# Odd tokens moved by a ladder matmul, and the diagonal block of a causal filter split in late and early outputs

## The reference, cut to what matters

```python
x = x + conv(_ln_c(x))                 # deformable 3x3 convolution, batch norm, SiLU; x is (4, 64, 32, 32)
t = _to_tokens(x)                      # (4, 1024 tokens, 64)
t = t + ffn(_ln_t(t))                  # spectral unit, below
x = _from_tokens(t, x)

# ffn, for u of (b, t, d), 16 filters phi_k, 4 branches over 1, 1/2, 1/4, 1/8 of the tokens
U_plus  = causal_conv(phi_k, u)        # by FFT in the reference
U_minus = (-1)^t * causal_conv(phi_k, (-1)^t * u)
out  = einsum('btkd,k,kde->bte', U_plus, s, Mpp) + einsum('btkd,k,kde->bte', U_minus, s, Mpm)
out += sum over lags 0..2 of u[t - lag] @ Mu[lag]
```

## Time and profile before

| | |
|---|---|
| median of 3 runs | 545.5 us (543.98 to 546.7) |
| the profiled execution | 545.57 us, of which the span of its records is 543.4 us |
| PE busy | 439.2 us, 81% of the span |
| DVE busy | 316.9 us, 58% |
| POOL busy | 296.8 us, 55% |
| ACT busy | 206.4 us, 38% |
| mean granted PE clock | 0.90 of 2.4 GHz |
| pass starts (L944 or first wait of the loop) | 110, 158, 208, 267, 332, 374, 425, 482 us; the end of the last is at 540 us |

### The profile page before, as it was taken

One profiled execution on the slowest core, in us unless ns is written; L12 is line 12 of the kernel. 1 busy time (PEld: TensorE's weight loads), 2 busy tenths in 40 slices (PEclk: granted clock), 3 DMA queues, 4 the chain that ended last, 5 costly groups with the idle time before them and its releaser, 6 DMA issues.

```text
span 543.4 us, 7147 instructions
## 1 busy us (share of the span) xinstructions
PE 439.2 (81%) x2660; PEld 217.9 (40%) x2660; DVE 316.9 (58%) x768; ACT 206.4 (38%) x413; POOL 296.8 (55%) x295
## 2 busy tenths in 40 slices
PE   4986481438775995999989996976699699989997
PEld 3442441315443442444434342643344354534333
DVE  5759977999864959292738429677374934040000
ACT  2124120125543562434333343654356244424232
POOL 1067777778777777777777773777776000000000
PEclk9999595558897999799989998889699889999999
DMA  6943699832334333333333332333433000000000
GB/s 154 185 109 106 155 326 349 259 111 83 102 102 112 102 98 109 103 104 103 104 109 98 104 100 53 104 93 108 114 103 97 6 10 1 2 5 11 0 1 10
DMA packets 47746, 54.41 MB, mean 100 GB/s; under 512 B 28656, under 2 KB 38134, under 8 KB 47713
## 3 DMA queue, kind: packets, MB, share of 16 engines
q0 software_dynamic: 13824, 37.77, 23.6%
q1 hardware_dynamic: 27865, 13.94, 10.2%
q10 hardware_dynamic: 6024, 2.26, 1.9%
HBM read 50.12 MB, written 3.30 MB: 98 GB/s over the span
## 4 chain that ended last, share of the span: by engine, by line
PE 58%; DVE 24%; DMA 10%; issue 3%; ACT 2%; SPq 1%; DVEq 0%
PE bank L902 32%; DMA u<-u 9%; PE bank L919 7%; PE bank L848 3%; PE bank L779 3%; DVE G L459 3%; PE bank L838 3%; DVE sil L472 2%; PE bank L760 2%; DVE G L460 2%; PE bank L939 2%; PE bank L876 1%; DMA filt<-in_L_ffn_phi_dram 1%; DVE V L463 1%; DVE st L299 1%
## 5 line engine op out<-in xcount | busy, mean ns | idle before, releaser
L279 POOL DMA_INDIRECT G<-corner_table,idx x288 | 294.2, 1022 | 122.0 <-issue 86.2
L902 PE MATMUL bank<-filt,u 128*128 128x512 f16 x960 | 243.2, 397 | 46.5 <-DMA u<-u 38.4
L680 ACT COPY u_conv<-bank 64x512 f32<-64x512 f32 x256 | 148.3, 579 | 202.7 <-PE bank L902 198.7
L902 PEld LDWEIGHTS bank<-filt,u 128*128 128x128 f16 x960 | 89.5, 100 | 167.8 <-issue 49.9
L919 PE MATMUL bank<-u_conv,mixw 128*64 128x256 f32 (+1 forms) x640 | 79.2, 356 | 5.9 <-issue 5.9
L459 DVE TENSOR_TENSOR G<-G,bank 128x2304 f32<-128x2304 f32 x32 | 81.5, 2547 | 1.3 <-DMA G<-corner_table,idx 1.2
L463 DVE TENSOR_TENSOR V<-G 128x576 f32<-128x576 f32 x32 | 24.4, 761 | 67.9 <-PE bank L839 67.2
L919 PEld LDWEIGHTS bank<-u_conv,mixw 128*64 128x64 f32 x640 | 35.8, 137 | 52.1 <-issue 50.6
L460 DVE TENSOR_TENSOR G<-G 128x1152 f32<-128x1152 f32 x32 | 43.5, 1358 | 1.1
L471 DVE TENSOR_SCALAR expo<-expo 128x128 f32<-128x128 f32 x16 | 4.4, 274 | 59.4 <-ACT expo L654 59.1
L838 PE MATMUL bank<-ident_swap,V 128*128 128x128 f32 x128 | 22.3, 309 | 14.6 <-DVE V L463 12.1
(11 more groups left out here) (153 smaller groups left out, 308.5 us busy)
## 6 DMA issues: line engine op xcount, KB each, us to landing
filt<-filter_rows SPq DMA_DIRECT2D x16, 514.0 KB, 12.2
G<-corner_table,idx POOLq DMA_INDIRECT x288
corner_table<-n_uT SPq DMA_DIRECT2D x12, 128.0 KB, 3.5
mixw<-in_x_dram SPq DMA_DIRECT2D x2, 512.0 KB, 6.3
filt<-in_L_ffn_M_phi_plus_dram SPq DMA_DIRECT2D x4, 256.0 KB, 7.5
out_dram<-o_sb ACTq DMA_DIRECT2D x8, 128.0 KB, 2.0
filt<-n_L_ffn_M_phi_minus_dram ACTq DMA_DIRECT2D x2, 256.0 KB, 5.6
corner_table<-n_uT ACTq DMA_DIRECT2D x4, 128.0 KB, 4.8
```

Source lines behind the costliest of these rows:

```text
L279: pool.indirect_dma_start(G[:, k, tap, :], None, corners[bp], bass.IndirectOffsetOnAxis(ap=idx[:, q % 2, k, tap:tap + 1], axis=0)).then_in ...
L680: act.copy(u_conv[C * par:C * par + C, g % 2, :, b2, p, :], conv_ps[par][rows].rearrange("c (k a) -> c k a", k=GROUP)).then_inc(conv_copie ...
L902: last = pe.matmul(conv_ps[par][:].rearrange("c (k a) -> c k a", k=GROUP), u16[:, NJ * bp + j2, hl, b2, par:par + 2].rearrange("s w c -> s ...
```

## The change

- **Moving the odd tokens.** The two SP DMAs and the memsets of slot 2 go. `ladder` is a 128x256 f16 matrix with an identity in columns 127 to 254 and zeros beside it, made by DVE at the start. In step 0 of a pass, ahead of the diagonal block, PE multiplies the chunk's odd tokens (and, for j > 0, those of the chunk before) with a slice of it: one or two matmuls of 256 columns into `conv_ps[1]`. ACT casts the result into slot 2 of `u16` (128x256), casts a 64x128 part into `u_early`, and copies 64x256 of `u16` into `u_early` as well. PE waits for the first two of these (`u_shifted`) ahead of all of step 1, and for the third (`early_ready`) inside step 2.
- **The order of steps.** `i` now gives group, then `par`, then image; the bank goes by the image, so that two steps in a row are the two images with the same filters.
- **The diagonal block.** It is triangular: the early 64 output tokens take nothing from the late 64 tokens. From step 2 on, the three diagonal matmuls of a step give only the 64 late outputs of each filter (256 columns, all 128 tokens). The early outputs of both images are made in the even step: three matmuls of 256 columns with the 64 early tokens of image 0 (partitions 64 to 127) into bank 0, each followed by one with the 64 early tokens of image 1, which `u_early` holds on partitions 0 to 63, into bank 1. The even step therefore waits in its middle for ACT to have emptied bank 1, and the odd step no longer waits for it. Steps 0 and 1 stay whole.

```diff
-            sp.wait_ge(shift_zeroed, BP)
-            for q in range(NQ):
-                sp.wait_ge(u_ready, 2 * q + 2)
-                sp.dma_start(u16[0:P - 1, q, :, :, 2], u16[1:P, q, :, :, 0]).then_inc(u_shifted, 16)
-                if q % NJ:
-                    sp.dma_start(u16[P - 1:P, q, :, :, 2], u16[0:1, q - 1, :, :, 0]).then_inc(u_shifted, 16)
...
-            for q in range(0, NQ, NJ):
-                dve.memset(u16[3 * P // 4:P, q, :, :, 2], 0.0).then_inc(shift_zeroed, 1)
+            dve.memset(ladder[:, 0:P - 1], 0.0)
+            dve.memset(ladder[:, 2 * P - 1:2 * P], 0.0)
...
+            dve.wait_ge(s_ident, 16)
+            dve.tensor_copy(ladder[:, P - 1:2 * P - 1], ident).then_inc(ladder_ready, 1)
...
-                g, b2, par = i // 4, i // 2 % 2, i % 2
+                g, par, b2 = i // 4, i // 2 % 2, i % 2
...
+            def copy_stepped(n):
+
+                act.wait_ge(u_stepped, n + 1)
+                stepped = conv_ps[1][:, 0:4 * C].rearrange("s (h b c) -> s h b c", h=2, b=2)
+                act.copy(u16[:, n, :, :, 2], stepped).then_inc(u_shifted, 1)
+                act.copy(u_early[:, :, 2], stepped[C:P, :, 1]).then_inc(u_shifted, 1)
+                act.copy(u_early[:, :, 0:2], u16[C:P, n, :, 1, 0:2]).then_inc(early_ready, 1)
+
             for n in range(NQ):
+                copy_stepped(n)
...
+                def step_odd_tokens():
+
+                    pe.wait_ge(u_ready, 2 * n + 2)
+                    pe.wait_ge(conv_copied[1], START + STEPS * n)
+                    dst = conv_ps[1][:, 0:4 * C].rearrange("s (h b c) -> s h b c", h=2, b=2)
+                    last = pe.matmul(dst, ladder[:, P:2 * P], u16[:, n, :, :, 0], start=True, stop=(j == 0))
+                    if j:
+                        last = pe.matmul(dst, ladder[:, 0:P], u16[:, n - 1, :, :, 0], start=False, stop=True)
+                    last.then_inc(u_stepped, 1)
...
-                    pe.wait_ge(conv_copied[par], START + STEPS * n + 2 * (i // 2))
+                    if not (split and b2):
+                        pe.wait_ge(conv_copied[b2], START + STEPS * n + 2 * (i // 2))
                     for j2 in range(j + 1):
                         if j2 == j and i == 0:
-                            pe.wait_ge(u_ready, 2 * n + 2)
-                        if j2 == j and i == 1:
-                            pe.wait_ge(u_shifted, 16 * (7 * bp + 2 * j + 1))
+                            step_odd_tokens()
+                        if j2 == 0 and i == 1:
+                            pe.wait_ge(u_shifted, 2 * (n + 1))
                         lag = P * (j - j2)
+                        a0 = C if split and j2 == j else 0
...
+                    if split and b2 == 0:
+                        if i == 2:
+                            pe.wait_ge(early_ready, n + 1)
+                        pe.wait_ge(conv_copied[1], START + STEPS * n + 2 * (i // 2))
+                        for e, (hl, part) in enumerate(products):
+                            last = pe.matmul(out_of[0][:, :, 0:C], u16[C:P, n, hl, 0, par:par + 2].rearrange("s w c -> s (w c)"),
+                                             filt_h[C:P, ks, par, part, 2:2 + C], start=False, stop=(e == 2), skip_group_check=True)
+                            pe.matmul(out_of[1][:, :, 0:C], u_early[:, hl, par:par + 2].rearrange("s w c -> s (w c)"),
+                                      filt_h[0:C, ks, par, part, 2 + C:2 + P], start=(e == 0), stop=False, skip_group_check=True)
```

More of the change, by code:

```diff
@@ L77, in metaformer_kernel @@
         off_bias = sb("off_bias", [P, NOFF])
+        ladder = sb("ladder", [P, 2 * P], F16)
+        u_early = sb("u_early", [C, 2, 3, C], F16)
         w_off = sb("w_off", [P, TAPS, NCH])
@@ L184, in metaformer_kernel @@
         conv_copied = [sem(f"conv_copied{i}") for i in range(2)]
-        shift_zeroed, u_shifted, mix_scaled = sem("shift_zeroed"), sem("u_shifted"), sem("mix_scaled")
+        early_ready = sem("early_ready")
+        ladder_ready, u_stepped, u_shifted, mix_scaled = sem("ladder_ready"), sem("u_stepped"), sem("u_shifted"), sem("mix_scaled")
         group_mixed, mixed_copied, pass_turned = sem("group_mixed"), sem("mixed_copied"), sem("pass_turned")
@@ L672, in copy_products @@
             def copy_products(n, i):
-                g, b2, par = i // 4, i // 2 % 2, i % 2
+                g, par, b2 = i // 4, i // 2 % 2, i % 2
                 if i % 4 == 0 and N_GROUPS * n + g >= 2:
                     act.wait_ge(group_mixed, N_GROUPS * n + g - 1)
-                act.wait_ge(conv_done[par], STEPS // 2 * n + i // 2 + 1)
+                act.wait_ge(conv_done[b2], STEPS // 2 * n + i // 2 + 1)
                 for p in range(2):
@@ L680, in copy_products @@
                     act.copy(u_conv[C * par:C * par + C, g % 2, :, b2, p, :],
-                             conv_ps[par][rows].rearrange("c (k a) -> c k a", k=GROUP)).then_inc(conv_copied[par], 1)
+                             conv_ps[b2][rows].rearrange("c (k a) -> c k a", k=GROUP)).then_inc(conv_copied[b2], 1)
             def store_pass(n):
@@ L862, in _ @@
             pe.wait_ge(ones_ready, 2)
+            pe.wait_ge(ladder_ready, 1)
             for r in range(2):
@@ L886, in _ @@
                           for s in range(seg0, seg0 + nseg)]
-                def convolve(i):
-                    g, b2, par = i // 4, i // 2 % 2, i % 2
+                def step_odd_tokens():
[6 more added lines that the diff above has]
+                    last.then_inc(u_stepped, 1)
+                def convolve(i):
+                    g, par, b2 = i // 4, i // 2 % 2, i % 2
+                    ks = slice(GROUP * g, GROUP * g + GROUP)
+                    products = ((0, 0), (0, 1), (1, 0))
+                    split = i >= 2
+                    out_of = [b[:].rearrange("c (k a) -> c k a", k=GROUP) for b in conv_ps]
                     if n == 0 and i % 4 == 0:
@@ L900, in convolve @@
                         lag = P * (j - j2)
-                        for e, (hl, part) in enumerate(((0, 0), (0, 1), (1, 0))):
-                            last = pe.matmul(conv_ps[par][:].rearrange("c (k a) -> c k a", k=GROUP),
+                        a0 = C if split and j2 == j else 0
+                        for e, (hl, part) in enumerate(products):
+                            last = pe.matmul(out_of[b2][:, :, a0:P],
                                              u16[:, NJ * bp + j2, hl, b2, par:par + 2].rearrange("s w c -> s (w c)"),
-                                             filt_h[:, GROUP * g:GROUP * g + GROUP, par, part, lag + 2:lag + 2 + P],
-                                             start=(j2 == 0 and e == 0), stop=(j2 == j and e == 2))
@@ L906, in convolve @@
-                    last.then_inc(conv_done[par], 1)
+                                             filt_h[:, ks, par, part, lag + 2 + a0:lag + 2 + P],
+                                             start=(j2 == 0 and e == 0 and not (split and b2)), stop=(j2 == j and e == 2), skip_group_check=True)
+                    if split and b2 == 0:
+                        if i == 2:
+                            pe.wait_ge(early_ready, n + 1)
+                        pe.wait_ge(conv_copied[1], START + STEPS * n + 2 * (i // 2))
+                        for e, (hl, part) in enumerate(products):
+                            last = pe.matmul(out_of[0][:, :, 0:C], u16[C:P, n, hl, 0, par:par + 2].rearrange("s w c -> s (w c)"),
+                                             filt_h[C:P, ks, par, part, 2:2 + C], start=False, stop=(e == 2), skip_group_check=True)
+                            pe.matmul(out_of[1][:, :, 0:C], u_early[:, hl, par:par + 2].rearrange("s w c -> s (w c)"),
+                                      filt_h[0:C, ks, par, part, 2 + C:2 + P], start=(e == 0), stop=False, skip_group_check=True)
@@ L908, in mix @@
+                    last.then_inc(conv_done[b2], 1)
                 def mix(k):
```

## The result

The changed kernel takes 505.34 us (median of four runs, 504.82 to 506.99), the kernel before beside it 545.71: ratio 0.9269, 95% interval 0.9236 to 0.9301, 7.3% faster. All ratios in this text are to the kernel before, run beside the version in question. The forecast was 504.4.

The account below looks back on a forecast made before the run. PE was taken as bound by the moved-token DMA (9.1% of the span, about 49 us) and the low clock behind it. Gathers cap the gain at 37.2 until pass 6, plus 3.95 behind: 545.57 - 41.15 = 504.4 us, range 500 to 516.

Parts of the forecast that it names:

- up to k=10 of pass 2: Passes 0 to 2: gathers hold k=10 of pass 2 to 240.3 against 248.66; 8.35 less 1.0 for clock, gain 7.35 us.
- starts of passes 3 to 7: Pass starts without the DMA wait, at full clock: gains 4.15, 5.35, 9.9, 6.55 and 1.25, sum 27.2 us.
- other pairs: Remaining step pairs with split diagonal: 0.9 us in rest of pass 2, 1.8 each in passes 3, 5, 6, 7; 8.1.
- rest of pass 4: Pass 4 after its start: no gain; pairs some 0.4 us longer, hidden by PE's 2.61 us wait for DVE at k=10.
- taken by the gathers at pass 6: k=10 of pass 6 not before 426.4, so gain there at most 37.2 against 38.7 us summed: gathers last by 1.5.
- The new chain: Pass start: PE may begin step 1 about 1.1 us after u_ready and step matmuls; 0.3 us waiting replaces the DMA.
- The pair: Two steps' diagonal: six 256-column matmuls 0.65 us plus half-row ones 0.32 side by side, against 1.30; 0.30 us saved per pair.
- rival 1: Half-row matmuls run one after the other, pairs save nothing: gain 33.3, 512.2 us; chance 0.17.
- The rule on weight loads: Skill page's 107 ns per 128-column load: six loads would fill 0.64 us and the pair save nothing; forecast sided against it.
- rival 2: Gathers hold more, POOL wins nothing back: k=10 of pass 6 at 434.2, gain 33.4, 512.2 us; chance 0.10.
- rival 3: Even step's wait for bank 1 bites with j = 1 and more: 0.5 us in 42 pairs, 21 us, 525; chance 0.06.
- rival 4: Small f16 matmuls cost 0.216 us each, pairs 1.3 dearer: 566 us, slower than before, deciding from 0.17 each; chance 0.03.

Follow-up runs that it names:

- e3_dma_order: Kernel before with only the new order of steps, keeping the DMA (waited for at step 2) and whole diagonal blocks: 526.21 us, ratio 0.9632.
- e8_ladder_old_order: Ladder alone, with steps and banks ordered as in the kernel before and whole diagonal blocks: 508.48 us, ratio 0.9301.
- e1_no_split: Changed kernel with ladder and new order, but whole diagonal blocks in all steps and no copies into u_early: 510.29 us, ratio 0.9343.
- e4_same_rows: Changed kernel with image 1's early half taken from the same 64 rows as image 0's: 515.69 us, ratio 0.9439.
- e7_filler: Changed kernel with unread filler matmuls on PE ahead of k=10 in passes 0, 1 and 4: 505.94 us, ratio 0.9279.
- e6_whole_j0: Changed kernel with whole diagonal blocks in passes 0 and 4: 503.26 us, ratio 0.9253.
- e11_after_again: The changed kernel itself, unedited, run again beside the later runs: 505.66 us, ratio 0.9255; its profiled execution took 507.28.
- e9_finish_first: Changed kernel with DVE's finish(q,0) moved ahead of weigh(q,1,1), so it doesn't stand behind the unit's last gathers: 496.53 us, ratio 0.9084.

## Why the prediction was right, and which of its steps were not

| term | forecast gain | in the two traces |
|---|---|---|
| up to k=10 of pass 2 | 7.35 | 7.74 |
| starts of passes 3 to 7 | 27.2 | 25.9 |
| other pairs | 8.1 | 5.6 |
| rest of pass 4 | 0 | -0.84 |
| taken by the gathers at pass 6 | -1.5 | 0 |
| sum | 41.15 | 38.4 |

The last column adds to 543.4 - 505.0. Forecast 504.4, profiled execution 506.99, median 505.34. The mechanism was right, and most of the gain lay where it was forecast. That the median came within 1 us is partly luck: between the two traces the sum was 2.75 us too high, with misses of both signs, and the profiled execution was the slowest of the four.

- **What bounds.** Right: the DMA's wait and the clock behind it were the two prices, and both fell. What I left out is that the new order alone would take more than a third of that wait (`e3_dma_order`). It changes no number of the forecast, since the ladder takes the whole wait either way (`e8_ladder_old_order`), but the prediction's text lets a reader believe that only the ladder touches it.
- **The new chain.** Forecast 1.1 us from `u_ready` and the step matmuls to step 1 and 0.3 us of waiting; measured 1.22 and 0.19. The third copy was covered.
- **Starts of passes 3 to 7.** Forecast 11.55, 4.75, 7.9, 8.95, 11.55; measured 11.92, 4.83, 7.80, 9.31, 11.92. The clock was as forecast. In passes 3, 6 and 7 some 0.37 is missing each time (the terms as written add to 11.50 and 8.91, so that 0.05 of my figures was a slip). In pass 3, 0.24 of it is the pair of steps 2 and 3 (265.60 to 270.72, 5.12 us, not 4.88) and 0.12 is step 1, whose twelve matmuls took 2.71 us (262.30 to 265.01), not 2.59.
- **The pair: the term that was mis-sized.** I took 0.108 us for a matmul of 256 columns, half of 0.216, and nothing for the change between full and half rows. The first was nearly right: they follow each other by 0.111. The second was not: the change costs 0.094 us in every even step, and that is most of what is missing. A pair of steps in pass 7 took 6.40 us against 6.60: 0.20 saved, not 0.30. The odd step gives 0.31 and the even one takes 0.11 back. The pair of steps 2 and 3, with the change back inside it, saves only 0.11 (5.12 us against 5.23 in `e1_no_split`). In the sum's 27 pairs that is 5.4; the traces have 5.6, and I had 8.1.
- **Side by side or one after another.** Side by side, by the starts within 0.01 us; `e4_same_rows` shows what rival 1 would have been, 515.7. Rival 1 had 512.2, with pairs that save nothing; in fact they lose, by the same mis-sizing (6.72 us in pass 7 of `e4_same_rows`, against 6.60 before).
- **The rule on weight loads.** Six loads of 128 f16 columns on half of the rows fitted beside matmuls that took about 0.34 us; the records of those at 267.99 run over 0.22 us in all. The Trainium skill, "TensorE: Matmul & The Clock Gate", section "LDWEIGHTS (loading the stationary operand)", puts 107 ns on each, which would fill 0.64 us. By that rule the traces don't agree. The same page, "Part 3: Packing small matmuls — row/col tiling", says that matmuls on different row groups run at once, and here it holds for two that share all their columns and differ in their banks, by the changed kernel beside `e4_same_rows`.
- **Passes 0 to 2.** k=10 of pass 2 was forecast for 240.3 and came at 240.92. The floor set by the gathers held: the last gather of (3,3) started at 221.96, DVE, which waited for it, went on 3.7 us later, at 225.69, and wrote last at 240.13; PE then arrived some tenths after that. For (2,3), a pass earlier, DVE was only 2.7 us behind the last gather, outside my 3.2 to 4.7. But the clock's 1.0 us stood in the wrong pass and was too small. It costs 2.8 us, behind the 7.48 us of waiting in pass 1 (`e7_filler`: 14.61 against 17.38), while pass 2 starts without loss, at 1.00. Pass 2 begins 1.1 us later than before (209.14 against 208.04), and its start wins all back.
- **Pass 4.** I set even steps 0.4 us longer and hid them behind PE's wait at k=10. Three of the four waits for bank 1 came as forecast, 0.41, 0.42 and 0.49 us, the first one was 0.77, and `e6_whole_j0` shows that they were hidden: without them k=10 came no sooner after the pass's start. The loss of 0.84 lies behind k=10, in the low clock behind a wait of 2.01 us, which I had not counted. It belongs to this execution and not to the kernel: in `e11_after_again` the clock stayed up there, and the rest of the pass took 12.1 us instead of 14.7.
- **The gathers at pass 6.** Forecast: k=10 not before 426.4, and the gathers last by 1.5 us. Measured: DVE's write at 426.58 and PE at 428.07:

```profile
415.58 2.56 DVE L458 TENSOR_TENSOR G<-G,bank 128x2304 f32<-128x2304 f32 x1 [6.78 <-DMA G<-corner_table,idx]
...
426.58 0.29 DVE L493 SCALAR_TENSOR_TENSOR u<-u_tok,u 128x128 f16<-128x128 f32 x1
...
428.07 0.49 PE L867 MATMUL bank<-ident_swap,u_tok 128*128 128x128 f32 x2
```

  The last gather was at 412.87, 2.2 us later than forecast, DVE began 2.7 us behind it, 1.2 sooner than the 3.9 I took, and its own work was 0.5 shorter, so its write came 0.5 us later than I had it. PE was the later one by 1.2 us, because it had saved less in its pairs. So this limit lay close, without deciding in this execution. It decided in `e11_after_again`: there PE waited for DVE at k=10 of pass 5 (1.36 us) and again, 0.20 us, at k=10 of pass 6, at 428.37, behind a last gather at 414.35, and what the clock had left it in pass 4 was gone by pass 6 (396.35 against 396.33). In `e7_filler`, where PE is earlier, the gathers bind at k=10 of pass 5 too.
- **Rivals 2 to 4.** POOL showed no long wait and its last gather moved from 418.44 to 412.87 (rival 2 wanted 418.44). Behind steps with j = 1 and more there is no wait for bank 1 (rival 3): all seven such waits, 3.6 us, lie in passes 0 and 4. The small matmuls cost 0.11 us, not the 0.17 of rival 4.

What stays open: why the clock fell behind 2.01 us of idling in one execution of the changed kernel and stayed behind 2.00 in another, why a change of rows costs 0.09 us, whether whole blocks would be better in passes 0 and 4, and whether gathers of more than one tap at a time would do better than the swap of `e9_finish_first`. The last wasn't tried.

## What to carry to other kernels

A DMA that waits on the path costs its wait and the slow matmuls behind it; count both, and expect that two edits that aim at the same wait don't add up. When the wait is gone, look at what the next engine does in front of the one that waits: the list of waits pointed at DVE, and swapping two calls there gave 1.8% more. Price small matmuls with what stands between them: here half-size matmuls cost nearly half, and the change between full and half rows took a third of the gain. And before an edit gets the credit for 2 us, see whether two executions of the same kernel differ by as much.

## What the runs showed of the hardware that was not expected

- Two f16 matmuls of 64 rows by 128 columns, 256 columns long, on different halves of the rows and into different banks start within 0.01 us of each other. Pairs follow 0.10 to 0.12 us apart; on the same rows each one alone takes that long.
- At full clock a matmul of 256 columns in a stream costs 0.111 us, one of 512 0.218. The first one on half of the rows behind one on all rows comes at least 0.09 us later than that, in each of 46 places; the change back, at which nothing was waited for, costs as much.
- Behind an idle stretch of 1.23 us the clock stayed at 2.4 GHz, behind 6.08 and 7.48 us it fell to 1.2 GHz, and behind 2.00 and 2.01 us, at the same place in two executions of the same kernel, it did either.
- DVE went on 2.7 us after the start of a block's last gather twice (174.33 to 177.05 and 412.87 to 415.58), and 3.7 us in between (221.96 to 225.69), where the trace before had 3.2 and 4.7.
